# Direction attention: second scores issued two heads at a time, each pair behind the exponential that read its banks

## The chip, the cores and the metric

The kernel runs on one core of a Trainium2 chip. The metric is the device time of one execution in microseconds; lower is better. The kernel before has a median of 2051.99 us over three runs (2046.13 to 2059.99).

## The reference, cut to what matters

The reference is a stack of four layers, each an attention-like block and a feed-forward block with a layer norm behind each. The change touches only the attention of layer 1 ("direction attention"): 8 heads, 4 sequences of 512 tokens in this program, 128 channels.

```python
scores = einsum(q3, k3) * scale + q_on_dir[..., :, None] * k_on_dir[..., None, :]
scores = where(causal, scores, -inf)
attn = softmax(scores)
out = einsum(attn, v) ... @ Wo.T
```

Queries and keys have three components a head and one along the head's direction. The kernel keeps them split into bf16 parts in 32 rows per head (`q_parts`, `k_parts`), so that one bf16 matmul with 32 rows gives an exact enough score.

## The kernel before, in words

The work is cut into **units** U = 0 to 7 (one sequence, four of the eight heads) and each unit into four **steps** k = 0 to 3, one for each tile of 128 keys; s = 4U + k counts the steps. The scores are computed twice. The **first scores** (queries on partitions, L1667, `first_products`, with a causal mask written before them by `first_mask`, L1662) serve only to find each query's maximum: VectorE reduces them in three pieces (`maxima`, L1812), and after four heads splits the maxima into bf16 parts (`split_maxima`, L1823). TensorE turns these into rows (`max_rows`, L1689), VectorE adds them to the queries (`less_maxima`, L1831), and then the **second scores** (keys on partitions, L1697, `second`) come out with the maximum already taken off, masked by a bf16 product of a mask and the identity (L1710).

ScalarE takes the exponential of the second scores in two instructions a step, one for heads 0 and 1, one for heads 2 and 3 (`probabilities`, L1772). TensorE multiplies the result with the values (`values`, L1714). The value tile has a column of ones, so the sums of the softmax come with it; `spread_sums` (L1725) spreads them, ScalarE inverts them (`inverse`, L1785), GpSimd normalises (L1658), and `out` (L1730) applies the output weights; VectorE adds the residual (L1836).

Second scores of step s have (4 - k) x 128 columns: 512, 384, 256, 128. Each of the four heads has one PSUM bank (2 to 5) for them, and there is one set of such banks, so the scores of step s+1 wait until the exponentials of step s have read them. First scores of the diagonal tiles use bank 0, the long pieces bank 1, values bank 6; bank 7 is shared by edge pieces, maximum rows, spread sums and output product, one after another (`m_read` holds what has to have read it).

The order on each engine is written out by hand. TensorE, in the loop at L1746: the second scores of step s+1, the first mask of head f = s + 7, then where they are due the output product (k = 0, odd U from 3), the maximum rows of the next unit (k = 1) or the spread sums of the last one (k = 2), then the values of step s and the first products of head f. The first products run seven heads ahead, so the last steps (from s = 25) have neither first mask nor products. In `second` the scores and masks of all four heads follow one wait for both exponentials of the step before (`probs_ready` at 2s); the semaphore `s_ready` goes up after the masks of head 1 and after those of head 3. There are no DMAs in this part.

The matmuls of `second` and `first_products` use 32 rows of the array (one head's group of rows), those of `values` 32 columns, and the masks, maximum rows, spread sums and output product all of it.

Of the kernel before, what the change touches and what calls it, by code (L numbers as in the profile page):

```python
# [1604 lines left out]
def direction_attention(core, q_parts, k_parts, v_aug, w_out, sum_spread):  # L1605
# [3 lines left out]
    H = 4  # L1609
    n_units = 2 * B  # L1610
    n_steps = n_units * QT
    n_heads = n_units * H
    LEAD = 7
    with Stage(core, "a1") as st:
# [20 lines left out]
        def diagonal_done(f):  # L1635
            return 3 * f + 1

        def long_done(f):
            return 3 * f + 2

        def edge_done(f):
            return 3 * f + 3

        def out_of(s):

            U, k = s // QT, s % QT
            return (U - 3) // 2 if k == 0 and U >= 3 and U % 2 == 1 else None

        with nc.Block() as block:
            @block.gpsimd  # L1650
            def _(pool):
                nc.gpsimd.memset(nparts[:], 0.0).then_inc(zeroed, 1)
                for U in range(n_units):
                    b, g = U // 2, U % 2
                    pool.wait_ge(inv_ready, U + 1)
                    if b > 0:
                        pool.wait_ge(out_done, b)
                    nc.gpsimd.tensor_tensor(yn[:, g, :], y[:, g, :], inv_sum[:], ALU.mult).then_inc(yn_ready, 1)  # L1658

            @block.tensor  # L1660
            def _(pe):
                def first_mask(f):  # L1662
                    if f >= 1:
                        pe.wait_ge(top_ready, diagonal_done(f - 1))
                    nc.tensor.matmul(ps_d, core.identb[:], mask_wide[:].rearrange("p q n -> p (q n)"), start=True, stop=False, skip_group_check=True)

                def first_products(f, m_read):  # L1667

                    U, h = f // H, f % H
                    col, g = (U // 2) * T, U % 2  # L1670
                    rows = slice(32 * h, 32 * h + 32)

                    def product(to, q, k, n):
                        return nc.tensor.matmul(to, q_parts[rows, g, col + q * P:col + (q + 1) * P], k_parts[rows, g, col + k * P:col + (k + n) * P],
                                                start=k != q, stop=True, skip_group_check=True)

                    for q in range(QT):
                        last = product(ps_d[:, q * P:(q + 1) * P], q, q, 1)
                    last.then_inc(first_ready, 1)
                    if f >= 1:  # L1680
                        pe.wait_ge(top_ready, long_done(f - 1))
                    product(ps_f[:, 0:2 * P], 2, 0, 2)
                    product(ps_f[:, 2 * P:4 * P], 3, 1, 2).then_inc(first_ready, 1)
                    if m_read is not None:
                        pe.wait_ge(*m_read)
                    product(ps_m[:, 0:P], 1, 0, 1)
                    product(ps_m[:, P:2 * P], 3, 0, 1).then_inc(first_ready, 1)

                def max_rows(U, m_read):  # L1689
                    pe.wait_ge(nparts_ready, U + 1)  # L1690
                    pe.wait_ge(*m_read)
                    for t in range(QT):
                        last = nc.tensor.matmul(ps_m[:, t * P:(t + 1) * P], nparts[:, t, :, :].rearrange("p h r -> p (h r)"), core.identb[:],
                                                start=True, stop=True)
                    last.then_inc(rows_ready, 1)

                def second(s):  # L1697
                    U, k = s // QT, s % QT
                    col, g = (U // 2) * T, U % 2
                    size = (QT - k) * P  # L1700
                    if k == 0:
                        pe.wait_ge(q_ready, U + 1)
                    if s > 0:
                        pe.wait_ge(probs_ready, 2 * (s - 1) + 2)
                    for h in range(H):
                        rows = slice(32 * h, 32 * h + 32)
                        nc.tensor.matmul(ps_s[:, h, 0:size], k_parts[rows, g, col + k * P:col + (k + 1) * P], q_less[rows, g, k * P:T],
                                         start=True, stop=False, skip_group_check=True)
                    for h in range(H):
                        last = nc.tensor.matmul(ps_s[:, h, 0:P], core.maskb[:], core.identb[:], start=False, stop=True, skip_group_check=True)  # L1710
                        if h % 2 == 1:
                            last.then_inc(s_ready, 1)

                def values(s):  # L1714
                    U, k = s // QT, s % QT
                    b, g = U // 2, U % 2
                    pe.wait_ge(probs_ready, 2 * s + 2)
                    if k == 0 and U > 0:
                        pe.wait_ge(y_ready, U)
                    for h in range(H):  # L1720
                        last = nc.tensor.matmul(ps_y[32 * h:32 * h + 32, k * P:T], v_aug[:, b * QT + k, H * g + h, :], probs_t[:, s % 2, h, 0:(QT - k) * P],
                                                start=k == 0, stop=k == QT - 1, skip_group_check=True)
                    last.then_inc(values_done, 1)

                def spread_sums(U, m_read):  # L1725
                    pe.wait_ge(y_ready, U + 1)
                    pe.wait_ge(*m_read)
                    nc.tensor.matmul(ps_m, sum_spread[:], y[:, U % 2, :], start=True, stop=True).then_inc(sums_ready, 1)

                def out(b, m_read):  # L1730
                    pe.wait_ge(yn_ready, 2 * b + 2)
                    pe.wait_ge(*m_read)
                    for g in range(2):
                        last = nc.tensor.matmul(ps_m, w_out[:, g, :], yn[:, g, :], start=g == 0, stop=g == 1)
                    last.then_inc(out_done, 1)

                pe.wait_ge(mask_ready, 1)
                m_read = None
                for f in range(LEAD):
                    first_mask(f)  # L1740
                    first_products(f, m_read)
                    m_read = top_ready, edge_done(f)
                max_rows(0, m_read)
                m_read = q_ready, 1
                second(0)
                for s in range(n_steps):  # L1746
                    U, k, f = s // QT, s % QT, s + LEAD
                    if s + 1 < n_steps:
                        second(s + 1)
                    if f < n_heads:  # L1750
                        first_mask(f)
                    if out_of(s) is not None:
                        out(out_of(s), m_read)
                        m_read = sum_done, out_of(s) + 1
                    if k == 1 and U + 1 < n_units:
                        max_rows(U + 1, m_read)
                        m_read = q_ready, U + 2
                    if k == 2 and U >= 1:
                        spread_sums(U - 1, m_read)
                        m_read = ln_ready, U  # L1760
                    values(s)
                    if f < n_heads:
                        first_products(f, m_read)
                        m_read = top_ready, edge_done(f)
                spread_sums(n_units - 1, m_read)
                out(B - 1, (ln_ready, n_units))
# [687 lines left out]
```

## Time and profile before

| what | value |
|---|---|
| median of three runs | 2051.99 us (2046.13 to 2059.99) |
| profiled execution, device time | 2053.46 us |
| its span, first to last instruction | 2051.7 us |
| TensorE busy | 1695.6 us, 83% |
| VectorE busy | 1137.3 us, 55% |
| ScalarE busy | 1118.9 us, 55% |
| GpSimd busy | 734.2 us, 36% |
| mean granted TensorE clock | 0.886 |

The totals cover all layers. Direction attention lies between 285 and 438 us; the loop that the change reorders starts with the first second scores at 301.6 us. In the tables, a granted clock of 1.00 is 2.4 GHz and 0.50 is 1.2 GHz; a number between them is the mean over a stretch. Times of a timeline are from the span's start.

### The profile page before, as it was taken

To read this page: it belongs to the slowest core of one execution; us is meant where nothing else is said; L and a number is where in the kernel's file an instruction comes from. 1 tells how busy PE (TensorE), PEld (TensorE's weight loads), DVE (VectorE), ACT (ScalarE), POOL (GpSimd) and SP (SyncE) were. 2 spreads that over 40 slices of the span, in tenths; PEclk is the share of its full clock that TensorE was granted. 3 is DMA by queue.
4 is the path that set the end of the run, shared out by engine and by line. 5 is a ranking of instruction groups with operands and counts; after the bars stand their busy time and mean duration, and the time that the engine had idled before them with its cause. 6 is when DMAs were issued, how large, how long until landed. Compare 5 with 4: busy or idle time off the path is not lost. (4 is left out here: it accounts for less than half of the span.)

```text
span 2051.7 us, 27897 instructions
## 1 busy us (share of the span) xinstructions
PE 1695.6 (83%) x8871; PEld 1087.0 (53%) x8888; DVE 1137.3 (55%) x2224; ACT 1118.9 (55%) x2343; POOL 734.2 (36%) x665
## 2 busy tenths in 40 slices
PE   5659778862999789999939999999959998757797
PEld 3337534331888456666515555555527885312685
DVE  4936564517666355555435555555546885542475
ACT  2324443441887445555446655555527887653596
POOL 1214320020333256666315555555313442000363
PEclk8869865775999899999979999999968999978898
DMA  1008100000211222222121111111007661000330
GB/s 32 1 13 183 33 4 1 1 21 22 97 62 52 77 52 57 62 61 54 31 74 45 42 43 42 41 42 42 23 12 256 210 223 45 19 8 19 103 115 24
DMA packets 52778, 120.28 MB, mean 59 GB/s; under 512 B 12724, under 2 KB 21660, under 8 KB 45468
## 3 DMA queue, kind: packets, MB, share of 16 engines
q1 hardware_dynamic: 52636, 118.55, 19.9%
q8 instruction: 69, 1.13, 0.2%
q14 instruction: 73, 0.60, 0.1%
HBM read 82.86 MB, written 2.10 MB: 41 GB/s over the span
## 5 line engine op out<-in xcount | busy, mean ns | idle before, releaser
L750 DVE TENSOR_TENSOR e_lo<-psum,e_hi 128x512 fp32r<-128x512 f32 x296 | 203.0, 686 | 87.0 <-ACT psum L715 87.0
L1343 ACT ACTIVATE h_probs<-psum,h_nmax 128x512 f32<-128x512 f32 (+3 forms) x256 | 132.6, 523 | 133.2 <-DVE h_nmax L1421 78.5
L673 PE MATMUL psum<-f_x_hi,f_w_hi 128*128 128x512 f32 x400 | 159.8, 399 | 38.6 <-PEq L843 36.1
L1421 DVE TENSOR_REDUCE h_nmax<-psum 128x1 f32<-128x512 f32 (+3 forms) x256 | 113.6, 486 | 119.3 <-PE psum L1232 119.3
L674 PE MATMUL psum<-f_x_hi,f_w_lo 128*128 128x512 f32 x400 | 159.0, 398 | 0.0
L675 PE MATMUL psum<-f_x_lo,f_w_hi 128*128 128x512 f32 x400 | 159.0, 397 | 0.0
L1158 POOL TENSOR_TENSOR h_swapped<-h_swapped,a2f_tables 128x512 f32<-128x512 f32 x64 | 81.7, 1276 | 200.4 <-DMA h_swapped<-h_raw 200.4
L715 ACT ACTIVATE psum<-psum,f_b 128x512 f32<-128x512 f32 x200 | 131.9, 660 | 30.1 <-PE psum L675 29.9
L692 PE MATMUL psum<-e_lo,f_w_hi 128*128 128x512 f32 x364 | 142.2, 391 | 1.9 <-POOL e_lo L641 0.9
L689 PE MATMUL psum<-e_hi,f_w_hi 128*128 128x512 f32 x364 | 142.2, 391 | 0.0
L690 PE MATMUL psum<-e_hi,f_w_lo 128*128 128x512 f32 x364 | 141.9, 390 | 0.0
L641 POOL TENSOR_TENSOR e_lo<-e_gated,e_hi 128x512 fp32r<-128x512 f32 x59 | 76.1, 1289 | 163.6 <-ACT e_hi L727 162.6
L1343 ACT ACTIVATE a_probs<-psum,a_nmax 128x512 f32<-128x512 f32 (+3 forms) x128 | 67.4, 527 | 119.5 <-DVE a_nmax L1421 70.9
L1158 POOL TENSOR_TENSOR a_swapped<-a_swapped,a_tables 128x512 f32<-128x512 f32 x64 | 81.9, 1280 | 116.1 <-DMA a_swapped<-a_raw 116.0
L635 POOL TENSOR_TENSOR sum_fm<-e_part,sum_fm 128x512 f32<-128x512 f32 x60 | 78.1, 1302 | 125.3 <-DVE e_part L776 92.6
L1229 PE MATMUL psum<-h_k,h_q 64*128 64x384 f32 (+3 forms) x512 | 105.1, 485 | 21.4 <-DVE h_p_t L1430 16.8
L1239 PE MATMUL psum<-ident,h_probs 128*128 128x128 f32 x640 | 109.2, 278 | 0.4 <-ACT h_probs L1343 0.4
L673 PEld LDWEIGHTS psum<-f_x_hi,f_w_hi 128*128 128x128 f32 x400 | 77.2, 193 | 57.5 <-issue 38.7
L1421 DVE TENSOR_REDUCE a_nmax<-psum 128x1 f32<-128x512 f32 (+3 forms) x128 | 62.6, 489 | 67.7 <-PE psum L1232 66.5
L1229 PE MATMUL psum<-a_k,a_q 128*128 128x512 f32 (+3 forms) x256 | 91.2, 438 | 7.7 <-POOL a_k L1163 7.7
L721 ACT ACTIVATE e_hi<-psum 128x512 fp32r<-128x512 f32 x128 | 76.6, 598 | 34.3 <-PE psum L675 34.3
L1257 PE MATMUL psum<-h_p_t,h_v 128*64 128x256 f32 (+3 forms) x512 | 89.9, 451 | 0.0
(425 smaller groups left out, 4135.6 us busy)
## 6 DMA issues: line engine op xcount, KB each, us to landing
e_gate<-gates SPq DMA_DIRECT2D x46, 1024.0 KB, 4.7
a_swapped<-a_raw SPq DMA_DIRECT2D x128, 128.0 KB, 2.3
h_swapped<-h_raw SPq DMA_DIRECT2D x256, 64.0 KB, 2.0
e_gate<-gates SPq DMA_DIRECT2D x16, 512.0 KB, 7.1
f_w<-in_l_experts SPq DMA_DIRECT2D x8, 512.0 KB, 5.6
f_w<-in_l_experts SPq DMA_DIRECT2D x32, 128.0 KB, 4.7
e_gate<-gates SPq DMA_DIRECT2D x12, 256.0 KB, 3.9
f_w<-in_l_experts SPq DMA_DIRECT2D x9, 256.0 KB, 4.9
```

Source lines behind the costliest of these rows:

```text
L673: nc.tensor.matmul(to, w_h, ex.x_hi[:, cols(b)], start=True, stop=False, skip_group_check=True)
L674: nc.tensor.matmul(to, w_l, ex.x_hi[:, cols(b)], start=False, stop=False, skip_group_check=True)
L675: nc.tensor.matmul(to, w_h, ex.x_lo[:, cols(b)], start=False, stop=True, skip_group_check=True).then_inc(hid_ready, 1)
L689: nc.tensor.matmul(to, w_h, hi[:, n % PLACES, :], start=start, stop=False, skip_group_check=True)
L690: nc.tensor.matmul(to, w_l, hi[:, n % PLACES, :], start=False, stop=False, skip_group_check=True)
L692: nc.tensor.matmul(to, w_h, lo[:, n % PLACES, :], start=False, stop=True, skip_group_check=True).then_inc(out_done, 1)
L715: nc.scalar.activation(to, hidden_bank(n), ex.act_func, **bias(n)).then_inc(act_ready, 1)
L750: nc.vector.tensor_tensor(lo[:, n % PLACES, :], whole, hi[:, n % PLACES, :].bitcast(F32), ALU.subtract).then_inc(lo_dve, 1)
L1158: nc.gpsimd.tensor_tensor(swapped[:, j, :], swapped[:, j, :], tables[:, 2 * j + 1, :], ALU.mult).then_inc(sin_ready, 1)
L1229: nc.tensor.matmul(ring[j % RING][:, 0:(q + 1) * P], qs[rows, U % 3, q * P:(q + 1) * P], ks[rows, U % 3, 0:(q + 1) * P], start=True, stop= ...
L1343: nc.scalar.activation(probs[:, j % 4, 0:(q + 1) * P], ring[j % RING][:, 0:(q + 1) * P], ACT.Exp, bias=nmax[:, j % 8:j % 8 + 1], accum_out ...
L1421: nc.vector.tensor_reduce(nmax[:, j % 8:j % 8 + 1], ring[j % RING][:, 0:(q + 1) * P], AX.X, ALU.max, negate=True).then_inc(max_ready, 1)
```

## The change

`second` gets a second argument, the pair p of heads, and does half of the work a call: the scores of two heads, their two masks, one count of `s_ready`. It waits for the exponential of the same pair of the step before in place of both. In the loop, pair 0 stands first, pair 1 behind the output product, maximum rows or spread sums; and the first mask moves from behind the second scores to just ahead of its first products, behind the values.

```diff
-                def second(s):
+                def second(s, p):
                     U, k = s // QT, s % QT
                     col, g = (U // 2) * T, U % 2
                     size = (QT - k) * P
-                    if k == 0:
+                    if k == 0 and p == 0:
                         pe.wait_ge(q_ready, U + 1)
                     if s > 0:
-                        pe.wait_ge(probs_ready, 2 * (s - 1) + 2)
-                    for h in range(H):
+                        pe.wait_ge(probs_ready, 2 * (s - 1) + p + 1)
+                    for h in range(2 * p, 2 * p + 2):
                         rows = slice(32 * h, 32 * h + 32)
                         nc.tensor.matmul(ps_s[:, h, 0:size], k_parts[rows, g, col + k * P:col + (k + 1) * P], q_less[rows, g, k * P:T],
                                          start=True, stop=False, skip_group_check=True)
-                    for h in range(H):
+                    for h in range(2 * p, 2 * p + 2):
                         last = nc.tensor.matmul(ps_s[:, h, 0:P], core.maskb[:], core.identb[:], start=False, stop=True, skip_group_check=True)
-                        if h % 2 == 1:
-                            last.then_inc(s_ready, 1)
+                    last.then_inc(s_ready, 1)
...
                 m_read = q_ready, 1
-                second(0)
+                second(0, 0)
+                second(0, 1)
                 for s in range(n_steps):
                     U, k, f = s // QT, s % QT, s + LEAD
                     if s + 1 < n_steps:
-                        second(s + 1)
-                    if f < n_heads:
-                        first_mask(f)
+                        second(s + 1, 0)
                     if out_of(s) is not None:
                         out(out_of(s), m_read)
                         m_read = sum_done, out_of(s) + 1
...
                     if k == 2 and U >= 1:
                         spread_sums(U - 1, m_read)
                         m_read = ln_ready, U
+                    if s + 1 < n_steps:
+                        second(s + 1, 1)
                     values(s)
                     if f < n_heads:
+                        first_mask(f)
                         first_products(f, m_read)
                         m_read = top_ready, edge_done(f)
```

## Rows read from the trace of the kernel before

**Rows 1.** Busy time by stretch: length, busy time (instructions) of each engine, granted clock, DMA

```profile
core 0: us, PE busy (x) PEld busy (x) DVE busy (x) ACT busy (x) POOL busy (x), PEclk, DMA share, GB/s
304.61:320.68 16.07, 14.18 (x102) 6.65 (x106) 6.83 (x16) 5.25 (x9) 0.00 (x0) 0.50 0.01 1
320.68:339.07 18.39, 16.40 (x106) 7.25 (x109) 8.22 (x19) 6.91 (x12) 1.26 (x1) 0.50 0.00 1
...
356.40:373.80 17.40, 14.31 (x109) 6.22 (x112) 8.89 (x20) 6.91 (x12) 1.26 (x1) 0.80 0.00 0
```

**Rows 2.** Waits of 301 to 430 us: total, times, longest

```profile
ACT a_probs_t L1777 <- PE psum L1710: 76.9, 32, 17.0
...
PEld psum L1693 <- DVE a_nparts L1829: 13.9, 7, 2.3
...
PEld psum L1707 <- ACT a_probs_t L1777: 8.0, 7, 2.1
...
PEld psum L1721 <- ACT a_probs_t L1777: 3.5, 5, 0.8
```

**Rows 3.** Timeline, first unit: start, us, engine line operation, count, idle before

```profile
304.61 0.51 PE L1707 MATMUL psum<-a_q_less,a1w_k_parts 32*128 32x384 bf16 x4 [1.82 <-ACT a_probs_t L1777]
305.05 0.61 PE L1710 MATMUL psum<-identb,maskb 128*128 128x128 bf16 x4
305.45 0.63 PE L1665 MATMUL psum<-a_mask_wide,identb 128*128 128x512 bf16 x1
...
306.01 1.94 PE L1721 MATMUL psum<-a_probs_t,a1w_v_aug 128*32 128x512 f32 x8
307.88 0.82 PE L1674 MATMUL psum<-a1w_k_parts,a1w_q_parts 32*128 32x128 bf16 x5
308.29 0.40 PE L1707 MATMUL psum<-a_q_less,a1w_k_parts 32*128 32x256 bf16 x3
...
308.92 0.42 PE L1707 MATMUL psum<-a_q_less,a1w_k_parts 32*128 32x256 bf16 x1
309.27 0.61 PE L1710 MATMUL psum<-identb,maskb 128*128 128x128 bf16 x4
```

**Rows 4.** Timeline at the turn to unit 3, all engines

```profile
354.09 0.40 PE L1710 MATMUL psum<-identb,maskb 128*128 128x128 bf16 x4
...
354.41 1.94 ACT L1777 ACTIVATE a_probs_t<-psum 128x1024 f32<-128x1024 f32 x2 [1.08 <-PE psum L1710]
...
356.23 0.60 ACT L1783 ACTIVATE a_y<-psum 128x512 f32<-128x512 f32 x1
356.40 0.34 PE L1707 MATMUL psum<-a_q_less,a1w_k_parts 32*128 32x384 bf16 x4 [0.63 <-ACT a_probs_t L1777]
356.68 0.40 PE L1710 MATMUL psum<-identb,maskb 128*128 128x128 bf16 x4
...
356.91 0.38 PE L1665 MATMUL psum<-a_mask_wide,identb 128*128 128x512 bf16 x1
...
357.24 1.95 PE L1734 MATMUL psum<-a_yn,a1w_w_out 128*128 128x512 f32 x4
```

**Rows 5.** Timeline, unit 3, around the maximum rows and the spread

```profile
363.45 0.40 PE L1693 MATMUL psum<-identb,a_nparts 128*128 128x128 bf16 x4 [2.16 <-DVE a_nparts L1829]
363.77 1.50 PE L1721 MATMUL psum<-a_probs_t,a1w_v_aug 128*32 128x384 f32 x8
...
366.89 0.63 PE L1665 MATMUL psum<-a_mask_wide,identb 128*128 128x512 bf16 x1
...
367.62 1.19 PE L1728 MATMUL psum<-a_y,a1w_sum_spread 128*128 128x512 f32 x1
```

**Rows 6.** Timeline of the tail

```profile
414.62 0.40 PE L1710 MATMUL psum<-identb,maskb 128*128 128x128 bf16 x4
414.86 1.92 PE L1728 MATMUL psum<-a_y,a1w_sum_spread 128*128 128x512 f32 x2
...
420.61 0.34 PE L1707 MATMUL psum<-a_q_less,a1w_k_parts 32*128 32x384 bf16 x4 [1.56 <-ACT a_probs_t L1777]
```

## The prediction

> **What bounds the kernel now.** I read the stage table first, then the waits of the stage, then TensorE's own timeline; the page's totals mix eight layers and say nothing of this one. Direction attention's steady part is six units and a tail between 301.6 and 428 us, 6% of the span. A unit (four key steps of four heads) takes 16.1 to 18.4 us, of which TensorE is busy 14.2 to 16.4, while VectorE is busy 7 to 9 and ScalarE 5 to 7 [rows 1]. So TensorE sets the pace. The reader should see the same in the waits: ScalarE waits 76.9 us for TensorE's second scores, but TensorE's matmuls of L1707 wait only 7 times for an exponential, 8.0 us by the weight loads (the matmuls behind them wait in the same pauses), and the values 3.5 us in 5 waits. The largest wait of TensorE in the stage is for VectorE's split maxima at L1693, 13.9 us in 7 waits, one per unit [rows 2]. The change attacks the smaller one.
>
> **What a step looks like.** In [rows 3], at the granted clock of 0.50 (the 1.2 GHz level, [rows 1]), four heads' scores start within a few hundredths of a microsecond of each other in one line ("x4"), because they sit in four different groups of 32 rows; 0.44 us later come the masks. Four masks of 128 columns take 0.40 to 0.43 us, so a column costs 0.00083 us and 384 columns 0.32: the scores stream once for all four, and 0.12 us is spent on going over to the full array. The same comes out at the 2.4 GHz level: 0.28 us less 384/512 of 0.23 is 0.11 [rows 4]. Going back is alike: the first mask (512 columns) is followed 0.56 us later by the values at the low clock and 0.33 us later at the high one, 0.13 and 0.10 above its columns [rows 3, 4]. I call 0.12 us a switch. Also, the scores of three heads start at 308.29 among the products of the fourth, and the fourth follows at 308.92: beside the products, second scores of other heads are free, and those of the products' own head cost their columns [rows 3].
>
> The trace has the switch between 32-row tiles and the full array at 0.12 us in these places. The Trainium skill, TensorEngine Tiling (Array Packing), Tiling Modes, Key Properties, says the same in kind ("Mode switching requires drain"), and gives no figure; by it alone each pair that is split off is charged, where a reading by matmul counts alone would give nothing. That rule speaks against this change, and the rows carry the price.
>
> **The change, part by part.**
> *Nothing is added in instructions:* same matmuls, masks, waits on VectorE, DMAs (none), and one more wait instruction per step. What changes is order. Pair 0 (heads 0, 1) of step s+1 goes first, then the output product, maximum rows or sum spread where there is one, then pair 1, values, the first mask, the products.
> *a. k=3, the 512-column scores of the next unit.* The products before them are of head 1, so pair 0 starts its masks where the four masks start today. Pair 1 now streams its 512 columns alone: 0.43 us low, 0.23 high, plus two switches, 0.24. Together 0.67 or 0.47. ScalarE doesn't gain: its first exponential starts 0.32 us after the first mask today [rows 4], which is pair 0's masks and latency, and the two exponentials then run 1.94 us on end. The second needs pair 1 by about 0.32 + 0.97 = 1.3 us; it comes at 0.9 (high) or 1.3 (low). No gain, no loss.
> *b. The first mask.* It leaves the place between masks and values, where one switch followed it, for the place between values and products, where there is one on both sides: +0.12 us, 0.12 at both levels.
> *c. k=0, 384 columns.* At the low clock TensorE arrives at these scores about when the exponential ends, so nothing is regained: pair 0 hides in the products of head 2, pair 1 streams where all four streamed before, plus two switches 0.24, plus b. At the high clock TensorE waits 0.63 us at 356.40 [rows 4]. After the change pair 1 still waits for that same second exponential; from 356.40 on, the old order runs 0.28 + 0.23 + 0.33 = 0.84 until the next work. The new one runs 0.16 + 0.12 + 0.12 + 0.12 = 0.52, but values wait for the copy of y (356.23 + 0.60, plus latency, 356.9 to 357.0), and the mask's 0.33 comes later: 0.93. With a. mostly absorbed by the 0.63 us wait, the pair a. and c. is worth about +0.1 us per unit at high clock. Where the output product stands there (three units), it runs inside the wait and in place of it: about -0.05. At the low clock a. to c. make 0.67 + 0.12 + 0.24 + 0.12 = 1.15 us.
> *d. k=1, the wait for the maxima.* This is the step I expect to decide. The wait of 2.16 us at 363.45 is for VectorE's chain that starts with the products, and it is what is left of that chain after all scores, the masks and the first mask have run beside it [rows 5]. The chain doesn't move. Afterwards only pair 0 runs beside it, and the wait grows to about 2.6 us (two masks 0.12, the first mask 0.23 and pair 1's share of columns 0.11 have left). Behind maximum rows there now follow pair 1 (256 columns, 0.21), its masks (0.21), two switches (0.24), and after the values the first mask with its switch, 0.56: 1.2 us per unit at the low clock, which is the clock there by the durations that follow (0.73 us from first mask to spread) [rows 5]. What is queued behind the waiting maximum rows is thus pair 1, values, products; ScalarE waits for pair 1 too, off the path.
> *e. k=2, the spread of the sums.* Pair 1's 128 columns, 0.11, and two switches, 0.24; the mask leaves a place where it cost 0.73 [rows 5] for one where it costs 0.56; without a mask ahead the spread follows 0.24 after the masks, their columns alone [rows 6]. Sum +0.18.
> *f. The tail (no products, from s = 25).* Six steps pay two switches each, 1.4, and the second streaming of a pair, some 0.8 together: at most +2.2. The waits there, 1.56 us at 420.61 [rows 6] and about 0.3 further on, could come back: at best -1.9. ScalarE's copy and inverse still stand in line behind pair 1's exponential, so I take +1.0, nearer the price of the switches.
>
> **Sum.** Units 1 and 2 at the low clock: 2 x 1.15 = 2.3. Units 3 to 6: 4 x 0.05 = 0.2. Step d six times 1.2 = 7.2, and once without a first mask, 0.67. Step e six times 0.18 = 1.1. Tail 1.0. Together **+12.5 us**. The profiled execution took 2053.46 us (span 2051.7), which would become 2066; it stands 1.5 us above the median of the three runs, 2051.99, which becomes **2064**. The unknown is what a switch costs back to 32-row tiles inside this stream: bounds 0 (hidden by weight loads running ahead) and 0.24 (twice the rows' value). Three more per step, less those that fall into waits, are 12 in units 1 and 2, 18 in step d, 12 in step e and 12 in the tail, 54 x 0.12 = 6.5 us, so the bounds move the sum by 6.5 either way.
>
> **Rivals.**
> *The waits win (faster).* If the split costs no switch and pair 0's early start lets ScalarE run ahead, the 8.0 + 3.5 = 11.5 us of waits go [rows 2], against some 4 us of columns streamed twice: -8, 2044. It decides if switches are under about 0.04 us. For it: the tail really is a ping-pong. Against it: in the units ScalarE's first exponential starts no earlier than today, and its wait of 76.9 us shows it isn't the bound.
> *It cancels.* Switches half hidden, d only 0.5 us each, the tail regained: 2052.
> *The clock tips down (clearly slower).* The granted clock is 0.50 in one unit of 18.39 us and 0.80 in one of 17.40 that holds an output product (1.87 us more) [rows 1]. TensorE's idle time in step d grows by the pair and the mask that no longer fill it (to about 2.6 us), and the stretch behind it is already at the low level. If units 3 to 6 fall to the low clock throughout, each costs 1.0 (18.39 less 17.40) to 2.9 us more (with the output product taken out), 1.8 in the middle, and a. to c. cost 1.15 in place of 0.05: 4 x 2.9 = 11.6 on top, +24, 2076. It decides if the 0.45 us of added idle in step d keeps the clock from coming back before the next unit. The Trainium skill, TensorE: Matmul & The Clock Gate, Part 1, What's actually happening, holds that "the default state is throttled, and activity releases the throttle"; no row tells how near units 3 to 6 stand to losing it. Against it: three switches per step are idle, but TensorE streams more columns too.
>
> **How the numbers follow.** Forecast 0.52, cancels 0.18, waits win 0.16, clock 0.14. The three runs differ by 14 us, so 1% (20.5 us) is about what tells a change from none. Range: 2046 (most of the way to the gain, less the run spread) to 2077 (the clock case). The forecast's own range is 2054 to 2072. Faster by over 1%, under 2031.5, is beyond all waits together: 0.02. Slower by over 1%, above 2072.5: most of the clock case, 0.10, and the forecast's upper end with every switch at 0.24, 0.03. Within: 0.85.
>
> **What would show it.** Right: the wait at L1693 grows from 2.16 to about 2.6 us per unit; masks come in "x2" pairs; 0.1 us gaps around pair 1; a low-clock unit of 16.07 us becomes 18.5; ScalarE's first exponential of a unit starts as long after the masks as before. Wrong: pair 1 follows pair 0's masks without a gap; the units get shorter; the wait at L1693 is filled by something else; the granted clock in 340 to 410 us leaves 0.7 to 0.8 in either direction.

## The result, and the profile after

The changed kernel takes 2071.51 us in the median of 11 runs (2061.32 to 2079.96), the kernel before 2050.42 us in 11 runs beside them (2046.13 to 2064.22). The ratio is 1.0085, 95% interval 1.0057 to 1.0114: slower by 0.85%, some 17 us (12 to 23), within 1% in the middle, while the interval reaches just over it. The ratio compares means; the medians are 21 us apart. The profiled executions took 2053.46 us before and 2076.33 us after, a pair 23 us apart, so a little further apart than the medians.

The difference is in direction attention. From the first second scores to the last spread of sums it takes 127.34 us before (301.64 to 428.98) and 148.92 us after (300.55 to 449.47), 21.6 us of the 22.9 us between the two profiles. Below I call this stretch the stage. The stage in the changed kernel, in the columns of [rows 1]:

```profile
300.55:449.47 148.92, 124.75 (x792) 46.90 (x792) 54.75 (x120) 55.11 (x86) 8.04 (x7) 0.67 0.00 1
```

TensorE is busy 124.75 us; before it was 104.35 us, at nearly the same mean granted clock (0.70 before, 0.67 after), with the same matmuls (the trace before lacks some of their records, 779 against 792). ScalarE and VectorE are as busy as before (55.11 and 54.75 us). The changed stage ends 20 us later, so its waits are taken from 285 to 460 us, to be laid beside [rows 2], which cover the whole stage before:

```profile
ACT a_probs_t L1778 <- PE psum L1710: 109.7, 45, 17.2
...
PEld psum L1693 <- DVE a_nparts L1830: 17.2, 7, 2.6
...
PEld psum L1707 <- ACT a_probs_t L1778: 6.8, 9, 1.2
...
PE psum L1727 <- DVE a_tops L1822: 4.1, 5, 1.2
...
PE psum L1733 <- DVE a_tops L1822: 2.1, 2, 1.3
...
PE psum L1707 <- ACT a_probs_t L1778: 0.8, 2, 0.5
```

One more line of the waits before, 301 to 430 us:

```profile
PE psum L1707 <- ACT a_probs_t L1777: 6.1, 7, 1.8
```

What the change was made for happened in part: the matmuls of the second scores wait 0.8 us in 2 waits for exponentials, where they waited 6.1 us in 7. Their weight loads still wait 6.8 us in 9 waits (8.0 in 7 before), 5.9 of it in the last 20 us, mostly beside other matmuls. ScalarE waits 109.7 us for TensorE where it waited 76.9, and two waits for VectorE have appeared that weren't in the list before, those of the spread of sums (L1727, 4.1 us in 5) and of the output product (L1733, 2.1 us in 2). A unit at the low clock, from the masks of the 512-column scores on, TensorE alone:

```profile
318.68 0.39 PE L1710 MATMUL psum<-identb,maskb 128*128 128x128 bf16 x2
319.00 0.61 PE L1707 MATMUL psum<-a_q_less,a1w_k_parts 32*128 32x512 bf16 x2
319.54 0.39 PE L1710 MATMUL psum<-identb,maskb 128*128 128x128 bf16 x2
319.87 0.66 PE L1720 MATMUL psum<-a_probs_t,a1w_v_aug 128*32 128x128 f32 x8
320.46 0.61 PE L1665 MATMUL psum<-a_mask_wide,identb 128*128 128x512 bf16 x1
321.00 0.82 PE L1674 MATMUL psum<-a1w_k_parts,a1w_q_parts 32*128 32x128 bf16 x5
```

The pairs are seen as "x2". From pair 1's scores to its masks takes the columns and a switch (319.00 to 319.54, 512 columns, 0.54 us), and from masks to scores again a switch (318.68 to 319.00, 0.32 us with 0.21 of masks). The first mask (320.46) now stands between values and products with its 0.54 us. Further on in the same unit:

```profile
325.66 0.82 PE L1674 MATMUL psum<-a1w_k_parts,a1w_q_parts 32*128 32x128 bf16 x5
...
329.19 0.61 PE L1693 MATMUL psum<-identb,a_nparts 128*128 128x128 bf16 x4 [1.96 <-DVE a_nparts L1830]
329.73 0.39 PE L1707 MATMUL psum<-a_q_less,a1w_k_parts 32*128 32x256 bf16 x2
...
330.38 1.51 PE L1720 MATMUL psum<-a_probs_t,a1w_v_aug 128*32 128x384 f32 x8
331.82 0.61 PE L1665 MATMUL psum<-a_mask_wide,identb 128*128 128x512 bf16 x1
332.36 1.03 PE L1674 MATMUL psum<-a1w_k_parts,a1w_q_parts 32*128 32x128 bf16 x6
...
333.64 0.39 PE L1710 MATMUL psum<-identb,maskb 128*128 128x128 bf16 x2
334.77 2.05 PE L1727 MATMUL psum<-a_y,a1w_sum_spread 128*128 128x512 f32 x2 [0.73 <-DVE a_tops L1822]
...
337.29 1.08 PE L1720 MATMUL psum<-a_probs_t,a1w_v_aug 128*32 128x256 f32 x8
...
340.45 0.39 PE L1710 MATMUL psum<-identb,maskb 128*128 128x128 bf16 x2
```

The same unit in the kernel before:

```profile
318.25 0.61 PE L1710 MATMUL psum<-identb,maskb 128*128 128x128 bf16 x4
319.21 0.66 PE L1721 MATMUL psum<-a_probs_t,a1w_v_aug 128*32 128x128 f32 x8 [0.36 <-DVE a_tops L1821]
...
324.13 0.82 PE L1674 MATMUL psum<-a1w_k_parts,a1w_q_parts 32*128 32x128 bf16 x5
...
327.66 0.61 PE L1693 MATMUL psum<-identb,a_nparts 128*128 128x128 bf16 x4 [1.54 <-DVE a_nparts L1829]
328.20 1.51 PE L1721 MATMUL psum<-a_probs_t,a1w_v_aug 128*32 128x384 f32 x8
329.64 1.03 PE L1674 MATMUL psum<-a1w_k_parts,a1w_q_parts 32*128 32x128 bf16 x6
```

The 0.36 us of idle time before the values at 319.21 are the first mask, whose record the trace lacks. From products to maximum rows it is 3.53 us in both (325.66 to 329.19, and 324.13 to 327.66 before): the chain on VectorE has not moved. Behind it stand pair 1 and its masks (329.73 to 330.38), and behind the values the first mask. From masks to the spread it is 1.13 us (333.64 to 334.77), though no first mask lies between them. The whole low unit takes 21.77 us (318.68 to 340.45) against 18.40 before (318.25 to 336.65).

### The profile page after: what moved, and what is told of

The parts are those of the page before. It is cut to its first block and busy times, and to the rows that moved or that the text cites. A ratio compares the mean times of both kernels' runs of the same rounds, so it can differ in the third digit from the quotient of the medians.

```text
span 2074.5 us, 27914 instructions
## 1 busy us (share of the span) xinstructions
PE 1711.6 (83%) x8888; PEld 1086.8 (52%) x8888; DVE 1142.7 (55%) x2224; ACT 1120.0 (54%) x2343; POOL 736.4 (35%) x665
## 3 DMA queue, kind: packets, MB, share of 16 engines
q1 hardware_dynamic: 52636, 118.55, 19.4%
q8 instruction: 70, 1.15, 0.2%
## 5 line engine op out<-in xcount | busy, mean ns | idle before, releaser
L1778 ACT ACTIVATE a_probs_t<-psum 128x1024 f32<-128x1024 f32 (+3 forms) x64 | 43.8, 704 | 109.8 <-PE psum L1710 109.7
```

## The experiments

All kernels were timed in five rounds beside the kernel before. Stage lengths and clocks are read as above, from one profile each; "low unit" is a unit at the 1.2 GHz level, from the masks of one 512-column step to those of the next.

| kernel | ratio to before (95%) | stage, us | stage clock |
|---|---|---|---|
| before | 1 | 127.34 | 0.70 |
| changed | 1.0085 (1.0057 to 1.0114) | 148.92 | 0.67 |
| e1 order of the pairs only | 1.0029 (1.0006 to 1.0053) | 135.92 | 0.68 |
| e2 first mask moved only | 1.0058 (1.0036 to 1.0081) | 136.75 | 0.69 |
| e3 pairs together, own waits | 1.0004 (0.9985 to 1.0023) | 123.52 | 0.78 |
| e4 changed, first mask early | 1.0155 (1.0136 to 1.0174) | 151.85 | 0.57 |
| e8 changed, filled | 1.0062 (1.0039 to 1.0084) | 138.59 | 0.75 |
| e9 before, filled | 0.9914 (0.9897 to 0.9930) | 109.05 | 0.92 |
| e6 rows behind values | 0.9931 (0.9910 to 0.9952) | 119.08 | 0.77 |
| e7 all three behind values | 0.9934 (0.9919 to 0.9950) | 114.93 | 0.82 |
| e12 changed, filled more | 0.9966 (0.9951 to 0.9981) | 121.01 | 0.93 |
| e11 pairs together, filled | 0.9930 (0.9904 to 0.9956) | 110.44 | 0.90 |
| e10 all behind values, filled | 0.9893 (0.9871 to 0.9915) | 106.76 | 0.92 |
| e13 rows behind values, filled | 0.9906 (0.9885 to 0.9928) | 111.26 | 0.88 |

### e1. The order of the pairs alone

```diff
-                    for h in range(H):
+                    for first in range(0, H, 2):
+                        for h in range(first, first + 2):
...
```

> Only the order of the second scores: scores of heads 0, 1, their masks, scores of heads 2, 3, their masks, still behind one wait for both exponentials, and nothing else moved. Theory (switches and columns streamed twice, where nothing covers them): a low-clock unit, from the masks of one 512-column step to those of the next, 18.4 us before, becomes 19.3 (+0.67 at k=3, +0.24 at k=0, nothing at k=1 and k=2, where VectorE is awaited anyway); the whole +7 us. Rival (the early release matters, order is free): 18.4 us and no change. Rival (all is the clock): low-clock unit 18.4, but longer low stretches.

The low unit took 19.27 us (316.90 to 336.17) against 19.3 expected and 18.40 before. TensorE's timeline of e1 at the turn to unit 1:

```profile
316.90 0.39 PE L1711 MATMUL psum<-identb,maskb 128*128 128x128 bf16 x2
...
317.76 0.39 PE L1711 MATMUL psum<-identb,maskb 128*128 128x128 bf16 x2
318.51 0.66 PE L1722 MATMUL psum<-a_probs_t,a1w_v_aug 128*32 128x128 f32 x8 [0.36 <-ACT a_probs_t L1778]
```

Masks to values are 1.61 us where they were 0.96 (318.25 to 319.21): +0.65 against +0.67. The step with 384 columns costs +0.23, those in front of VectorE's waits 0.00 and 0.03. The price of switches and of columns streamed twice is thus shown step by step at the low clock. The whole was +0.29%, +1 to +11 us, where 7 were expected.

### e2. The first mask alone

```diff
-                    if f < n_heads:
-                        first_mask(f)
                     if out_of(s) is not None:
...
                     if f < n_heads:
+                        first_mask(f)
                         first_products(f, m_read)
```

> The kernel before with only the first mask moved to behind the values, ahead of its products; second scores undivided. Theory amended by the trace (the first mask filled waits for VectorE at k=1 and, unseen, at k=2): low-clock unit 19.7 us (+0.54 at k=1 and k=2, +0.12 at the other two), the whole +8 us. As predicted before the result: +0.12 at k=2 too, low-clock unit 19.3, the whole +5. Rival (the mask's place doesn't matter): 18.4 and no change.

Its profile has no unit that is low throughout, but the steps can be read at the low clock one by one. The line that tells the two versions of the theory apart is the spread, in TensorE's timeline of e2:

```profile
330.14 0.60 PE L1710 MATMUL psum<-identb,maskb 128*128 128x128 bf16 x4
331.27 2.05 PE L1728 MATMUL psum<-a_y,a1w_sum_spread 128*128 128x512 f32 x2 [0.52 <-DVE a_tops L1820]
```

Masks to spread are 1.13 us although the mask has gone; before they were 1.12 with it. Timeline of the kernel before, unit 1, TensorE and VectorE:

```profile
330.93 0.61 PE L1710 MATMUL psum<-identb,maskb 128*128 128x128 bf16 x4
...
331.32 0.63 PE L1665 MATMUL psum<-a_mask_wide,identb 128*128 128x512 bf16 x1
...
331.49 0.42 DVE L1821 TENSOR_REDUCE a_tops<-psum 128x2 f32<-128x256 f32 x1
...
332.05 2.04 PE L1728 MATMUL psum<-a_y,a1w_sum_spread 128*128 128x512 f32 x2
```

The spread writes bank 7 and must wait for the third piece of VectorE's maxima there; that ends at 331.49 + 0.42 = 331.91, and the spread starts 0.14 us later. The first mask had been lying in that wait. Moved behind the values it costs its full 0.54 us at k=2 as at k=1 (values to products 1.98 in place of 1.44 there), and 0.12 at k=3. The whole rose by 0.58%, 7 to 17 us, which holds the 8 of the amended theory at its lower end and not the 5 of the prediction's steps.

### e3. Both pairs where all four stood

```diff
                     if s + 1 < n_steps:
                         second(s + 1, 0)
+                        second(s + 1, 1)
+                    if f < n_heads:
+                        first_mask(f)
...
-                    if s + 1 < n_steps:
-                        second(s + 1, 1)
                     values(s)
                     if f < n_heads:
-                        first_mask(f)
```

> Pairs with their own waits, back to back where all four stood, the first mask in its old place; so e1 with the early release. Theory: the release is worth little, as ScalarE cannot start earlier: low-clock unit 19.3 as in e1, whole +6 against +7 of e1, the difference from the tail. Rival (the waits win): 3 to 8 us faster than e1, so at or below the kernel before.

It came out level with before (-3 to +5 us), against +6 expected, and 5 us under e1, though their intervals overlap. At the low clock its steps are those of e1 to the hundredth (masks to values 1.61 us, 319.21 to 320.82): there the early release gives nothing. At the high clock it does. From the masks of the 512-column scores to the products of k=0, where no output product stands, e1 takes 4.49 us and e3 4.02:

```profile
409.43 0.28 PE L1711 MATMUL psum<-identb,maskb 128*128 128x128 bf16 x2
...
413.92 0.50 PE L1674 MATMUL psum<-a1w_k_parts,a1w_q_parts 32*128 32x128 bf16 x5
```

```profile
337.53 0.28 PE L1710 MATMUL psum<-identb,maskb 128*128 128x128 bf16 x2
...
341.55 0.50 PE L1674 MATMUL psum<-a1w_k_parts,a1w_q_parts 32*128 32x128 bf16 x5
```

The first two lines are from e1, the others from e3; the kernel before takes 4.13 (405.89 to 410.02). So splitting costs 0.36 us there and the release returns 0.47. With an output product in between both take 6.41 us, and the release returns nothing. The result lies where the rival "the waits win" had put it, and part of its gain may also be the clock: 0.78 in its profile against 0.68, though one profile of each doesn't show that. Its unit at the high clock, the first seen, took 13.12 us.

### e4. The changed kernel with its first mask ahead of the waits

```diff
                     if s + 1 < n_steps:
                         second(s + 1, 0)
+                    if f < n_heads:
+                        first_mask(f)
...
                     values(s)
                     if f < n_heads:
-                        first_mask(f)
                         first_products(f, m_read)
```

> The changed kernel with only the first mask put back ahead of the output product, maximum rows and spread: pair 0, first mask, those, pair 1, values, products. Theory: it returns the 1.3 us a unit that e2 costs: low-clock unit 20.4 against 21.6 of the changed kernel, the whole +11 against +17. Rival (placing pair 1 behind the waits is all of the loss): as the changed kernel, +17 or more.

This is the largest miss. The low unit was 20.47 us, as expected (20.4), 1.3 us better than the changed kernel's. Yet the whole was +1.55%, 28 to 36 us, where 11 were expected. The stage of e4, in the columns of [rows 1]:

```profile
299.96:451.81 151.85, 131.06 (x780) 51.20 (x792) 54.75 (x120) 56.22 (x86) 8.06 (x7) 0.57 0.00 1
```

The granted clock is 0.57: its units (20.47, 20.48, 21.73, 20.47, 23.74 us) had 0.50, 0.50, 0.66, 0.50 and 0.57, where those of the changed kernel reach 0.80 and 0.92 and those of the kernel before 0.80. All five of its executions had a lower mean clock over the whole kernel (0.877 to 0.883) than any of the 25 of the kernel before beside them (0.884 to 0.902). So what an order costs isn't only its steps. Which clock the stage gets is worth as much as the whole change.

### e8 and e9. Filling the wait

```diff
+                    if k == 1 and f < n_heads:
+                        for _ in range(4):
+                            first_mask(f)
                     if k == 1 and U + 1 < n_units:
                         max_rows(U + 1, m_read)
```

This is e8; in e9, the kernel before, it is three times.

> The changed kernel, in which the first mask of a head is also written four times more ahead of the maximum rows (k=1), into the bank that it fills again later; TensorE would stand idle there for VectorE. No order that matters changes; the extra 4 x 0.43 us (low) or 4 x 0.22 us (high) fit into the wait of 1.96 to 2.38 us. Clock theory (beyond its own price the change lowers the clock, through TensorE's idle time): granted clock of the stage above the 0.67 of the changed kernel, low-clock unit still 21.5 us, the whole +3 to +12 against the kernel before in place of +17. Theory without the clock: stage clock and whole as for the changed kernel, +17.

> The kernel before with three more writes of the first mask in the wait for the split maxima (k=1), 3 x 0.43 us into 1.5 us or 3 x 0.22 us into 2.2 us. Clock theory: stage clock above 0.70, the whole 5 to 15 us faster than before. Theory without the clock: no change.

The kernel before gained 0.86%, 14 to 21 us, by 18 superfluous matmuls (three in each of six units). The stage of e9, in the columns of [rows 1]:

```profile
302.52:411.57 109.05, 89.37 (x809) 38.84 (x809) 54.70 (x120) 54.05 (x86) 8.06 (x7) 0.92 0.00 1
```

And TensorE's timeline of its third unit:

```profile
330.02 0.40 PE L1710 MATMUL psum<-identb,maskb 128*128 128x128 bf16 x4
...
334.15 0.61 PE L1674 MATMUL psum<-a1w_k_parts,a1w_q_parts 32*128 32x128 bf16 x6
...
335.33 1.04 PE L1665 MATMUL psum<-a_mask_wide,identb 128*128 128x512 bf16 x4
337.47 0.40 PE L1693 MATMUL psum<-identb,a_nparts 128*128 128x128 bf16 x4 [1.10 <-DVE a_nparts L1832]
...
343.25 0.40 PE L1710 MATMUL psum<-identb,maskb 128*128 128x128 bf16 x4
```

The extra writes (L1665 x4, at 335.33) lie ahead of the maximum rows, which come 3.32 us after the products start (334.15), as at 360.13 to 363.45 before; nothing on VectorE's chain moved. But the unit from 330.02 to 343.25 takes 13.22 us (it is all at the high level), against 18.40 at the low one. Writing full-array matmuls into TensorE's idle time raised the stage's clock from 0.70 to 0.92. The other executions agree: the mean clock over the whole kernel was 0.901 to 0.911 in the six of e9 and 0.887 to 0.897 in the eleven of the kernel before beside them. The Trainium skill, TensorE: Matmul & The Clock Gate, Part 1, What's actually happening, says that "the default state is throttled, and activity releases the throttle"; this pair agrees in direction, and e4 (TensorE busy 86% of the stage, clock 0.57) shows that the busy share by the records doesn't tell it. A low clock raises that share by itself, as four masks take 0.40 us at the low level and 0.23 at the high one. In the changed kernel four writes brought less: a stage clock of 0.75 and a ratio of 1.0062, 8 to 17 us, where 3 to 12 were expected by the clock theory and 17 by the other. The interval overlaps with the changed kernel's, and only one profile's stage (138.59 for 148.92) points to a gain, so e8 decides nothing by itself.

### e6 and e7. The values into the wait

```diff
+                    values(s)
                     if out_of(s) is not None:
                         out(out_of(s), m_read)
...
-                    values(s)
```

The diff is that of e7, with all three behind the values; in e6 only `max_rows` stands behind them.

> The kernel before with the maximum rows (k=1) moved behind the values of that step, so that the values fill the wait for VectorE. Theory (TensorE's order round VectorE's chain is what counts): values of 1.44 us (low) or 0.78 us (high) go into the wait, the products' edge pieces wait some 0.3 us more; low-clock unit 18.4 to about 17.2, the whole -7 us, more where the clock rises. Rival (the products behind the rows now wait for the new maxima and the head start is lost): 18.4 and no change.

> The kernel before with output product, maximum rows and spread all behind the values. Theory: e6, and the spread's wait of about 0.3 us for VectorE at k=2 goes too, as far as the products' edge pieces don't wait for the logarithm in its place: low-clock unit about 17.0, the whole -9 us. Rival (bank 7 is now handed on too late at k=0 and k=2): worse than e6.

Both gain, 0.69% and 0.66%, some 14 us each and more than the 7 and 9 us of the steps; the stage's clock was 0.77 and 0.82 with them. Neither profile has a unit that is low throughout, so the expected low units of 17.2 and 17.0 us were not seen. They can't be told apart in time, so the extra step of e7 isn't shown to bring anything by itself.

### e12. The changed order at the high clock

```diff
+                    if f < n_heads and (k in (1, 2) or out_of(s) is not None):
+                        for _ in range(5 if k == 1 else 2):
+                            first_mask(f)
                     if out_of(s) is not None:
                         out(out_of(s), m_read)
```

> The changed kernel with the first mask written five times more in the wait at k=1, twice more ahead of the spread (k=2) and of the output product, so that TensorE hardly stands idle for VectorE. Counted from high-clock steps of the traces so far, the changed order costs 1.5 us a unit more than the old one at the high clock and 2.7 us with an output product, 11.5 us in all. If the clock is then high as in the filled kernel before (stage clock about 0.9), theory: the whole about 2034 + 12 = 2046, that is -2 to -8 against the kernel before and 12 above the filled one. Rival (split and moved mask cost nothing once the clock is high): 2034. Rival (what lowers the clock is not idle time but the many turns to 32-row matmuls): stage clock still near 0.7, the whole +12.

The whole took 2045.96 us (12 runs), -0.34%. The stage's clock is 0.93, so the many turns to 32-row matmuls do not keep the clock down where the waits are filled. With both orders at the high level, the change can be priced without the clock. TensorE's timeline of e12:

```profile
331.99 0.29 PE L1710 MATMUL psum<-identb,maskb 128*128 128x128 bf16 x2
...
343.59 1.10 PE L1727 MATMUL psum<-a_y,a1w_sum_spread 128*128 128x512 f32 x2 [0.41 <-DVE a_tops L1825]
...
346.76 0.28 PE L1710 MATMUL psum<-identb,maskb 128*128 128x128 bf16 x2
```

The unit is 14.77 us (331.99 to 346.76) against 13.22: +1.55, expected 1.5. It is made up of 0.09 in a to c, 0.75 in d and 0.70 in e. With an output product it is 17.88 against 15.17: +2.7, as expected. The extra writes delay nothing: maximum rows start 3.32 us after the products in both, and the spread 1.49 us after the masks. The stage is 11.96 us longer than the filled kernel before, and the ratios differ by 0.52%, 11 us.

### e11. Pairs together, filled

> The pairs back to back with their own waits and the first mask in its old place (the earlier experiment), with three more writes of the first mask in the wait at k=1. Its only all-high unit took 13.12 us against 13.22 of the filled kernel before. Theory (at the high clock the early release just pays for the split): within 3 us of the filled kernel before, about 2034. Rival (the release wins where ScalarE is the slower one): 2028. Rival (the split costs): 2042.

The edit is e3 with the three writes of e9. The stage is within 1.4 us of e9 (110.44 and 109.05), at a clock of 0.90; all-high units take 13.11 and 13.22 us. The median, 2038.99 us, lies nearer to the rival that the split costs (2042) than to the theory (2034); its interval (0.9904 to 0.9956) overlaps with that of e9. In an all-high unit split and early release together bring 0.1 us: the release pays for the split and little more.

### e10 and e13. A version that beats both

> The kernel before with output product, maximum rows and spread behind the values, and two more writes of the first mask between values and maximum rows. Theory: both gains add where the clock stays high: a unit of 13.2 us loses 0.78 us at k=1 and up to 0.57 at k=2, about 12.0; the whole about 2026, 8 below the filled kernel before. Rival (the values had filled the wait well enough, what is added only delays): 2038 as without filling.

> The same with only the maximum rows behind the values. Theory: a unit of 12.4 us at the high clock, the whole about 2029. Rival as there: 2037.

The edits are e7 and e6 with two writes of the first mask between values and maximum rows. e10 takes 2032.34 us, 0.9893 (0.9871 to 0.9915), the fastest of all: 1.1% under the kernel before and 1.9% under the changed one. Its all-high unit is 12.47 us where 12.0 were expected and 13.22 is e9; the whole was 6 us above the 2026 expected. By the intervals it isn't told apart from e9 and e13. e13 took 2034.63 us where 2029 were expected. None of its units was high throughout: three had a clock of 0.88 and took 14.12 to 14.30 us, so the 12.4 us expected at the high clock were not seen.

## Why the prediction was right, and where it was wrong

The forecast, slower by 12.5 us and within 1%, held: 2064 forecast, 2071.51 measured, inside 2046 to 2077. Against the interval of 12 to 23 us, 12.5 is at the lower end, since two of its terms were too small. Step by step, at the clock for which each was worked out:

| step | predicted, us | measured, us |
|---|---|---|
| a to c, low clock | 1.15 | 1.10 (0.23 + 0.54 - 0.21 + 0.54) |
| a to c, high clock, no output product | 0.1 | 0.09 |
| a to c, high clock, with output product | -0.05 | 1.26 |
| d, maximum rows, low clock | 1.2 | 1.19 (0.65 + 0.54) |
| e, spread, low clock | 0.18 | 1.08 (0.54 + 0.54) |
| f and the last step d | 1.7 | 0.9 (16.57 less 15.64, the clock changing within both) |

The four terms of the low-clock a to c are masks to values, values to products, products to values and values to products, each read from the two timelines (318.25 to 324.13 before, 318.68 to 325.66 after). The two of the high clock are from masks to the products of k=0: 4.22 us after (386.36 to 390.58) and 4.13 before, and 7.33 after (403.29 to 410.62) and 6.07 in the filled kernel before (343.25 to 349.32).

**Right:** TensorE sets the pace and ScalarE's wait is no bound [rows 1, 2]; a switch costs 0.12 us [rows 3] and is charged in front of and behind pair 1, as e1 shows alone; VectorE's chain stays and what stood ahead of it goes behind (d). ScalarE's first exponential of a unit starts 0.33 us after the masks (386.36 to 386.69), as the 0.32 before. The prediction held the release of the banks for worthless at the low clock, and e1 and e3, whose low steps agree, show it. At the high clock it expected the split to be mostly absorbed in TensorE's wait; e1 and e3 show that it is the release that does this, by 0.47 us where no output product stands.

**The step that was mis-sized is e, and with it the output product in c.** The prediction took the 0.73 us from first mask to spread [rows 5] for the mask's own price. It was the mask plus what was left of a wait for bank 7: VectorE must have read its third piece of maxima there. So the mask's place was free, as at k=1, and moving it cost 0.54 us. Pair 1 behind the spread cost another 0.54, where 0.35 had been charged (0.11 + 0.24), because its two masks, 0.21 us, no longer lay in that wait either. Together that is 1.08 in place of 0.18, and over six units 5.4 us. The output product goes through the same bank, and a row of it was misread in the same way. The prediction took the 0.33 us from first mask to the next matmul at 356.91 [rows 4] for columns and a switch. But what follows is the output product, which uses the whole array like the mask, and VectorE was reading its third piece (timeline of the kernel before, VectorE):

```profile
356.68 0.42 DVE L1821 TENSOR_REDUCE a_tops<-psum 128x2 f32<-128x256 f32 x1
```

That ends at 357.10, and the output product starts 0.14 us later, at 357.24. The switch back at the high clock is 0.09 by other rows (332.85 to 333.16 in e9, less 0.22 of columns), so its size stands. Before, the output product had 0.84 us of work ahead of it [rows 4]; now it has only pair 0's scores and masks, and it waits up to 1.26 us. Timeline of the changed kernel at the turn to unit 5, TensorE and VectorE:

```profile
404.73 0.50 PE L1674 MATMUL psum<-a1w_k_parts,a1w_q_parts 32*128 32x128 bf16 x5
...
405.38 0.29 PE L1710 MATMUL psum<-identb,maskb 128*128 128x128 bf16 x2
...
406.36 0.42 DVE L1822 TENSOR_REDUCE a_tops<-psum 128x2 f32<-128x256 f32 x1
...
406.93 1.95 PE L1733 MATMUL psum<-a_yn,a1w_w_out 128*128 128x512 f32 x4 [1.26 <-DVE a_tops L1822]
...
409.30 1.06 PE L1720 MATMUL psum<-a_probs_t,a1w_v_aug 128*32 128x512 f32 x8
```

Here too it starts 0.15 us after VectorE's read of bank 7 ends (406.78). The prediction had it "inside the wait". From these products to the values is 4.57 us here and 4.08 in the filled kernel before (344.24 to 348.32), +0.49 where the prediction counted on a gain. The rest of the 1.26 us is pair 1 in place of the mask at k=3 (0.13) and the moved mask at k=3 and k=0 (0.32 each). Two such turns at 1.31 us more than forecast are 2.6 us. With the measured prices in the prediction's own sum: 2 x 1.10 + 2 x 0.09 + 2 x 1.26 + 6 x 1.19 + 6 x 1.08 + 0.9 = 19.4 us, against 21.6 between the profiled stages and 12 to 23 by the interval of the runs. (By its own terms the prediction's line for units 3 to 6 is 0.1 us, not 0.2.)

That 19.4 comes so near to 21.6 is in part luck, because the sum takes d and e at the low clock in all six units. In the changed profile two of the six steps d ran at the high one, where e12 prices them at 0.75 and e at 0.70. By unit, from masks to masks, the changed kernel is slower by 1.5, 3.4, 4.0, 7.0, -0.1 and 1.9 us, and by 3.8 in the tail: the 7.0 is a turn at 0.55 that before was at the high clock, the -0.1 a unit at 0.80 that before had 0.70. What is shown without the clock is 3.37 us for a low unit, and 1.55 (2.7 with an output product) for a high one.

**The clock rival** was named with 0.14 and a price of 11.6 us, as falling to the low level. Its mechanism is real and may have been priced too small: e4 lost 21 us beyond its steps by the runs (32 less 11) and 13 by the profiled stages (24.5 less 11), and e9 gained 17 by the reverse. In the change as made, the mean clock fell only from 0.70 to 0.67. Its share of the 21.6 us is not separated: 2 us are left over the sum at low prices, 10 over the 12.0 us that the same change costs with both orders filled. Between 340 and 410 us the clock was 0.68, and 0.76 before; the prediction had named leaving 0.7 to 0.8 as a sign of being wrong, and it was just left. The wait at L1693 did grow, from 2.16 to 2.38 us at the high clock, where 2.6 had been named as the sign.

**Open:** why e4, which is less idle than the changed kernel (14% of the stage against 16%), gets the lower clock. It doesn't turn between kinds of tile more often: its first mask stands beside pair 0's masks, and in the changed kernel and e12, which is high, it stands between values and products. No run here tells which share of the filling's gain comes from the time filled and which from the full-array matmuls that fill it. Full-array matmuls are not needed for all of it: e6 and e7 fill a wait with the values, which use 32 columns, and their six executions each had a mean clock of 0.897 to 0.907 over the whole kernel, the kernel before beside them 0.887 to 0.897.

## What to carry to other kernels

Before moving work off a place in a queue, ask what it was covering there: a short gap after it (0.73 us for 0.43 us of columns) may be the rest of a wait on another engine, and the move then costs the full price of the work. Splitting a group of row-tiled matmuls costs its columns again and a switch on each side, so it pays only where the waiting that it ends is longer and on the bounding engine, as e3 does against e1 at the high clock. And where TensorE's granted clock hovers between its levels, compare orders at the same level first, and try to fill its waits, with useful work if there is any, before reordering anything.

## What had not been expected of the hardware

Eighteen superfluous matmuls of 512 columns, in waits of 1.5 to 2.2 us, made the kernel 0.86% faster by raising the stage's granted clock from 0.70 to 0.92. One order of the same matmuls (e4) had a clock of 0.57 with TensorE busy 86% of the time, where the kernel before had 0.70 with 82%. And matmuls on other groups of 32 rows overtake those of a busy group: scores of three heads start at 308.29, ahead of three products (308.49) that stand before them in TensorE's order [rows 3]; in the changed kernel the scores of pair 0 do the same (326.07 ahead of 326.28).
